# A decoder layer with an SSM branch on one core: the short convolution folded into the input projection on TensorE, the first projections placed ahead of it, and SP's queue reordered

## The reference, cut to what matters

```python
h  = layernorm(x)                        # 4 x 256 x 256
q, k, v = h @ Wq.T, h @ Wk.T, h @ Wv.T   # 32 query heads, 8 key heads of 64
q, k = rope(q), rope(k)
attn = softmax(causal(q @ k.T / 8)) @ v
x1 = x + attn @ Wo.T
# SSM branch on the context: 256 inner channels e
p  = in_proj_w @ ctx.T                   # 256 x 1024
xc[e, t] = sum(conv_w[e, j] * p[e, t - 3 + j] for j in range(4))   # within a sequence
u  = silu(xc + conv_b)
dt, Bm, Cm = split(x_proj_w @ u)         # 8, 16, 16 rows
delta = softplus(dt_proj_w @ dt + dt_proj_b)
state[e, n] = state[e, n] * exp(-exp(A_log) * delta) + delta * u * Bm[n]
y = sum_n(state * Cm) + D * u            # gated with silu(layernorm(x1)), added to x1
out = x2 + gated_ffn(layernorm(x2))      # 704 hidden channels, integer weights
```

## Time and profile before

| what | us |
|---|---|
| median of 3 runs | 524.07 (522.26 to 529.78) |
| the profiled execution | 523.78 |
| its span, first to last instruction | 522.0 |
| PE busy | 414.5 (79%) |
| DVE busy | 366.6 (70%) |
| ACT busy | 271.0 (52%) |
| POOL busy | 221.3 (42%) |
| mean granted TensorE clock | 0.912 of full |

### The profile page before, as it was taken

How to read it: one execution, slowest core, us unless ns; L and a number is a source line. 1 busy time by engine, 2 the same in 40 slices (tenths; PEclk the granted TensorE clock), 3 DMA queues, 4 the chain that set the end, 5 groups by cost and what they waited for, 6 DMA issues and landing times.

```text
span 522.0 us, 7681 instructions
## 1 busy us (share of the span) xinstructions
PE 414.5 (79%) x2604; PEld 325.4 (62%) x2636; DVE 366.6 (70%) x485; ACT 271.0 (52%) x779; POOL 221.3 (42%) x234
## 2 busy tenths in 40 slices
PE   3648987188768697987889799978998894659996
PEld 1433666166656476866777688757887773447774
DVE  2774357257999885897798679858767999755442
ACT  0514587046556465755666658645556665433321
POOL 1741232206464666446446635635464474310000
PEclk9787789687889799998999989989999997779999
DMA  9325324703151415201430521323042130000000
GB/s 223 74 56 96 113 51 131 230 10 98 37 170 55 156 31 153 96 11 46 133 102 24 144 91 48 76 87 102 21 133 74 57 102 0 2 0 21 20 22 20
DMA packets 51110, 40.63 MB, mean 78 GB/s; under 512 B 32280, under 2 KB 43744, under 8 KB 51072
## 3 DMA queue, kind: packets, MB, share of 16 engines
q1 hardware_dynamic: 40864, 34.48, 23.2%
q0 software_dynamic: 4096, 4.20, 3.4%
q10 hardware_dynamic: 6112, 1.47, 1.4%
HBM read 26.36 MB, written 1.18 MB: 53 GB/s over the span
## 4 chain that ended last, share of the span: by engine, by line
PE 33%; DVE 17%; issue 15%; SPq 12%; POOL 9%; DMA 7%; ACT 5%; ACTq 2%; DVEq 0%; POOLq 0%
PE ps_s L1041 6%; SPq L303 6%; PE ps_p L1028 6%; PE ps_p L1243 5%; DMA qt<-rc 4%; POOL rc L418 4%; DVE state L793 4%; PE ps_s L1228 3%; DVE nmax L711 3%; PE ps_p L1141 3%; PE ps_r L1095 3%; DVE state L786 3%; DMA kt<-rc 3%; SPq L266 2%; POOL y L424 2%
## 5 line engine op out<-in xcount | busy, mean ns | idle before, releaser
L493 ACT ACTIVATE prob<-ps_s,nmax 128x256 f32<-128x256 f32 (+1 forms) x256 | 104.8, 444 | 72.6 <-DVE nmax L711 72.6
L424 POOL TENSOR_TENSOR y<-y,state 128x1024 f32<-128x1024 f32 x32 | 80.3, 2510 | 112.2 <-DVE state L799 112.2
L418 POOL TENSOR_TENSOR rc<-rc,rs 128x512 f32<-128x512 f32 x40 | 57.7, 1442 | 104.0 <-DVE rs L699 70.4
L711 DVE TENSOR_REDUCE nmax<-ps_s 128x2 f32<-128x512 f32 (+1 forms) x96 | 60.3, 682 | 45.1 <-PE ps_s L1052 45.1
L499 ACT ACTIVATE pt<-ps_r 128x512 f32<-128x512 f32 x96 | 53.6, 593 | 58.1 <-PE ps_r L1095 54.5
L793 DVE TENSOR_TENSOR_SCAN state<-decay,state 128x1024 f32<-128x1024 f32 x32 | 81.5, 2546 | 2.3 <-ACT decay L519 1.2
L1041 PE MATMUL ps_s<-kt,qt 64*128 64x256 f32 (+1 forms) x512 | 55.5, 360 | 30.7 <-DMA qt<-rc 30.7
L1028 PE MATMUL ps_p<-xt_all,wq 128*128 128x256 f32 x256 | 71.2, 427 | 9.1 <-DVE rs L703 6.4
L1041 PEld LDWEIGHTS ps_s<-kt,qt 64*128 64x128 f32 x512 | 47.1, 201 | 38.2 <-DMA qt<-rc 32.5
L266 POOL DMA_DIRECT2D qt<-rc x128 | 63.8, 504 | 9.7 <-POOL rc L418 9.5
L1141 PE MATMUL ps_p<-wo,attn_t 128*128 128x256 f32 x256 | 61.7, 389 | 7.7 <-DVE x L816 4.1
(11 more groups left out here) (110 smaller groups left out, 531.1 us busy)
## 6 DMA issues: line engine op xcount, KB each, us to landing
bc<-bc_scratch SPq DMA_DIRECT2D x32, 512.0 KB, 4.7
qt<-rc POOLq DMA_DIRECT2D x128, 32.0 KB, 1.7
qt<-rc SPq DMA_DIRECT2D x128, 32.0 KB, 2.0
kt<-rc SPq DMA_DIRECT2D x64, 32.0 KB, 1.8
kt<-kt SPq DMA_DIRECT2D x8, 256.0 KB, 3.0
wo<-wo_t SPq DMA_DIRECT2D x1, 2048.0 KB, 10.9
wq<-wqkv_t SPq DMA_DIRECT2D x24, 64.0 KB, 2.6
xs<-x SPq DMA_DIRECT2D x1, 1024.0 KB, 8.1
```

Source lines behind the costliest of these rows:

```text
L418: nc.gpsimd.tensor_tensor(rc[:, r % 2, :, :], rc[:, r % 2, :, :], rs[:], ALU.add).then_inc(rope_add, 1)
L424: nc.gpsimd.tensor_tensor(y[:, v % 2, :], y[:, v % 2, :], state[:, v % 2, :], ALU.add).then_inc(state_free, 1)
L493: nc.scalar.activation(o, i, ACT.Exp, bias=nmax[:, r, c:c + 1], accum_out=rsum[:, r, GRP + head:GRP + head + 1]).then_inc(exp_done, 1)
L711: nc.vector.tensor_reduce(nmax[:, u % 2, c:c + k], ps_s[:, part, :].rearrange("p (k s) -> p k s", k=k), AX.X, ALU.max, negate=True).then_i ...
```

## The change

The four-tap convolution and the in-projection are both linear, so their weights are multiplied beforehand. POOL fills a matrix `ones` (instead of clearing the pad of the removed buffer). DVE scales the identity by each tap's weight (`diag`, 8 instructions of 128 x 128), PE multiplies `ones` by it, which puts each channel's tap weight in every row (2 matmuls of 512 columns, `row_ps`), and DVE multiplies that into the in-projection's weights (`taps`, 8 instructions). PE then convolves with four accumulating matmuls a bank, over the context shifted by 0 to 3 positions (16 matmuls of 506 to 512 columns), and ACT takes u straight from PSUM, with the bias, in four pieces of 512 columns. The in-projection, its copies, and the convolution on DVE and POOL go.

PE's order is now: tables, rows, x(0), x(1), k(0), q(0), x(2), x(3), conv(0), q(1), conv(1), v(0), scores(0), then as before. ACT's queue has `par` ahead of the tables and the eight pieces of wq behind the first activation. The k moves are shared, four issues by SP and four by POOL; the doubling is a step of its own (`double_k`), behind the next q move. SP's loop starts at unit 0, spreads the feed-forward loads over the units 4 to 8 and 11, and takes B and C for the scans of the unit before. On DVE, `prepare_scan(u)` runs ahead of the unit's scans; the dequantisations move to the units 10 and 14.

```diff
+        taps = early[:, 0:EB * DC * P].rearrange("p (e j n) -> p e j n", e=EB, j=DC)
+        diag = early[:, L:L + EB * DC * P].rearrange("p (e j n) -> p e j n", e=EB, j=DC)
+        ones = early[:, 2 * L:2 * L + P]
...
@@ sync
+            def double_k(j):
+
+                sp.wait_ge(k_sp[j % 2], 16 * k_moves * (j // 2 + 1))
+                sp.wait_ge(k_pool[j % 2], 16 * k_moves * (j // 2 + 1))
+                sp.dma_start(kt[HD:P, j % 2, :, :], kt[0:HD, j % 2, :, :]).then_inc(k_in[j % 2], 16)
...
-            move_k(0)
-            move_q(0)
-            move_q(1)
+            move_k(sp, 0, range(KG // 2), k_sp)
+            move_q(sp, 0, range(GRP // 2), q_sp)
+            double_k(0)
+            move_q(sp, 1, range(GRP // 2), q_sp)
...
             load_bc(0)
-            move_q(2)
-            load_wq(sp, 6)
-            load_wq(sp, 7)
-            move_q(3)
-            move_k(1)
-            sp.dma_start(wo[:], wo_t.rearrange("(k p) n -> p k n", p=P)).then_inc(wo_in, 16)
-            sp.dma_start(wgu_i[:], wgate_t.rearrange("(k p) n -> p k n", p=P)).then_inc(ffn_in, 16)
...
-            move_q(4)
-            move_q(5)
-            sp.wait_ge(ssm_ready, 5)
-            load_bc(1)
-            for u in range(4, UNITS):
+            for u in range(UNITS):
                 if u + 2 < UNITS:
-                    move_q(u + 2)
-                if u % KG == 1 and u // KG + 1 < GROUPS:
-                    move_k(u // KG + 1)
-                for v in scans(u):
+                    move_q(sp, u + 2, range(GRP // 2), q_sp)
+                if u % KG == 2 and u // KG + 1 < GROUPS:
+                    double_k(u // KG + 1)
+                if u < 2:
+                    load_wq(sp, 6 + u)
+                if u == 2:
+                    sp.dma_start(wo[:], wo_t.rearrange("(k p) n -> p k n", p=P)).then_inc(wo_in, 16)
+                load_ffn(u)
+                for v in scans(u - 1) if u else ():
                     if v % 2 == 1 and v // 2 + 2 < NS:
                         sp.wait_ge(hc_done, v + 1)
...
+                        load_bc(v // 2 + 2)
+                if u % KG == 1 and u // KG + 1 < GROUPS:
+                    move_k(sp, u // KG + 1, range(KG // 2), k_sp)
+                if u == 3:
+                    sp.wait_ge(ssm_ready, 5)
+                    load_bc(1)
...
@@ gpsimd
             add_rope(("k", 0))
+            move_k(nc.gpsimd, 0, range(KG // 2, KG), k_pool)
             add_rope(("q", 0))
...
                 if u % KG == 1 and u // KG + 1 < GROUPS:
                     add_rope(("k", u // KG + 1))
+                    move_k(nc.gpsimd, u // KG + 1, range(KG // 2, KG), k_pool)
...
@@ scalar
+            def silu_u(e):
+
+                for h in range(2):
+                    act.wait_ge(conv_ps, 2 * e + h + 1)
+                    src = ps_r[:, h, :] if e == 0 else ps_o[:] if h == 0 else ps_s[:, 2, :]
+                    nc.scalar.activation(u_s[:, e, h * 512:(h + 1) * 512], src, ACT.Silu,
+                                         bias=par[:, e, DC:DC + 1]).then_inc(u_done, 1)
...
@@ vector
+            for e in range(EB):
+                for j in range(DC):
+                    nc.vector.tensor_scalar(diag[:, e, j, :], ident[:], par[:, e, j:j + 1], None, ALU.mult
+                                            ).then_inc(diag_done, 1)
             dve.wait_ge(ln_rstd, 1)
...
+            for e in range(EB):
+                dve.wait_ge(row_ps, e + 1)
+                dve.wait_ge(ctx_in, 32)
+                for j in range(DC):
+                    nc.vector.tensor_tensor(taps[:, e, j, :], ps_s[:, e, j * P:(j + 1) * P],
+                                            inproj[:, e * P:(e + 1) * P], ALU.mult).then_inc(taps_done, 1)
             dve.wait_ge(tab_sb, 4)
             rope(("k", 0))
             rope(("q", 0))
-            convolve(0, slice(B // 2, B), conv_done0, DC)
             rope(("q", 1))
-            convolve(1, slice(B // 2, B), conv_done2)
             negmax(0)
...
+                if u < 4:
+                    prepare_scan(u)
                 for v in todo[:1]:
                     drive(v)
                     scan(v)
...
-                if u < 4:
-                    prepare_scan(u)
-                if u == 5:
+                if u == 10:
                     dequantise_gate()
-                if u == 12:
+                if u == 14:
                     dequantise_up_down()
...
@@ tensor
+            for e in range(EB):
+                pe.wait_ge(diag_done, DC * (e + 1))
+                nc.tensor.matmul(ps_s[:, e, :], ones, diag[:, e, :, :].rearrange("p j n -> p (j n)"),
+                                 start=True, stop=True).then_inc(row_ps, 1)
+
+            def convolve(e):
+
+                pe.wait_ge(taps_done, DC * (e + 1))
+                pe.wait_ge(ctx_in, 32)
+                pe.wait_ge(xt_sb, B)
+                for h in range(2):
+                    o = ps_r[:, h, :] if e == 0 else ps_o[:] if h == 0 else ps_s[:, 2, :]
+                    o = o.rearrange("p (b s) -> p b s", b=2)
+                    src = ctxs[:, h * 512:(h + 1) * 512].rearrange("p (b s) -> p b s", b=2)
+                    for lag in range(DC):
+                        last = nc.tensor.matmul(o[:, :, lag:], taps[:, e, DC - 1 - lag, :], src[:, :, 0:S - lag],
+                                                start=(lag == 0), stop=(lag == DC - 1))
+                    last.then_inc(conv_ps, 1)
...
                 if u == 0:
-                    pe.wait_ge(inp_sb, 2 * EB)
+                    pe.wait_ge(u_done, 2 * EB)
...
+            transpose_x(0)
+            transpose_x(1)
             fill(("k", 0))
             fill(("q", 0))
+            transpose_x(2)
+            transpose_x(3)
+            convolve(0)
             fill(("q", 1))
+            convolve(1)
             fill(("v", 0))
             scores(0)
```

More of the change, by code:

```diff
@@ L188, in decoder_layer @@
         wv_in = sem("wv_in")
-        q_in = [sem(f"q_in{r}") for r in range(2)]
-        k_half = [sem(f"k_half{r}") for r in range(2)]
+        q_sp = [sem(f"q_sp{r}") for r in range(2)]
+        q_pool = [sem(f"q_pool{r}") for r in range(2)]
+        k_sp = [sem(f"k_sp{r}") for r in range(2)]
+        k_pool = [sem(f"k_pool{r}") for r in range(2)]
         k_in = [sem(f"k_in{r}") for r in range(2)]
@@ L250, in load_wq, with move_q @@
                                         ).then_inc(wq_in[g], 16)
-        q_moves, k_moves = 2 * GRP, 2 * KG
-        half_moves = q_moves // 2
-        q_low = [sem(f"q_low{r}") for r in range(2)]
-        def move_heads(queue, u, heads, landed):
+        q_moves, k_moves = GRP, KG
+        def move_q(queue, u, heads, landed):
             r = ROPE_AT["q", u]
@@ L267, in move_heads, with move_k @@
                                     ).then_inc(landed[u % 2], 16)
+        def move_k(queue, j, heads, landed):
+            r = ROPE_AT["k", j]
+            queue.wait_ge(rope_add, r + 1)
+            if j >= 2:
+                queue.wait_ge(score_done, 3 * KG * (j - 1))
+            for i in heads:
+                for c in range(2):
+                    queue.dma_start(kt[c * HALF:(c + 1) * HALF, j % 2, i, :],
+                                    rc[i * HALF:(i + 1) * HALF, r % 2, c, :]).then_inc(landed[j % 2], 16)
         block = ctx.enter_context(nc.Block())
@@ L308, in _, with load_bc @@
-            move_k(0)
-            move_q(0)
-            move_q(1)
+            def double_k(j):
+                sp.wait_ge(k_sp[j % 2], 16 * k_moves * (j // 2 + 1))
+                sp.wait_ge(k_pool[j % 2], 16 * k_moves * (j // 2 + 1))
+                sp.dma_start(kt[HD:P, j % 2, :, :], kt[0:HD, j % 2, :, :]).then_inc(k_in[j % 2], 16)
+            def load_bc(n):
+                for c in range(2):
+                    sp.dma_start(bc[:, n % 2, c, :], bc_scratch[c * NS + n:c * NS + n + 1, :].to_broadcast([P, L])
+                                 ).then_inc(bc_in[n % 2], 16)
@@ new lines, in _, with load_ffn @@
+            full = P * (HT - 1)
+            def load_ffn(u):
+                if u == 4:
+                    sp.dma_start(wgu_i[:], wgate_t.rearrange("(k p) n -> p k n", p=P)).then_inc(ffn_in, 16)
+                elif u == 5:
+                    sp.dma_start(wdn_i[:, 0:HT - 1, :], wdown_t[0:full, :].rearrange("(k p) n -> p k n", p=P)
+                                 ).then_inc(ffn_in, 16)
+                    sp.dma_start(sdn[:], s_down.rearrange("(a n) -> a n", a=1).to_broadcast([P, HID])
+                                 ).then_inc(ffn_in, 16)
+                elif u == 6:
+                    sp.dma_start(wdn_i[0:HP[-1], HT - 1, :], wdown_t[full:HF, :]).then_inc(ffn_in, 16)
+                elif u in (7, 8):
+                    i, v = (0, s_gate) if u == 7 else (1, s_up)
+                    with nc.allow_non_contiguous_dma(reason="704 scales, once"):
+                        sp.dma_start(sgu[:, i, 0:HT - 1], v[0:full].rearrange("(k p) -> p k", p=P)
+                                     ).then_inc(ffn_in, 16)
```

(18 more changed lines are left out.)

111 lines of the change are left out of this document (22 added, 89 removed).

## The result

The kernel after took 485.22 us (median of 4 runs, 481.47 to 489.71) against 523.84 for the kernel before on the same chip: 0.922 of its time, 95% interval 0.912 to 0.932. Run again in five rounds it took 484.91 us, ratio 0.927 (0.923 to 0.932). The forecast was 497, with a range of 484 to 510: the sign is right, and the gain was forecast 12 us too small.

A forecast was written before the change was run, and what follows sets the result against it. No engine was full; TensorE's 30.7 us of waits for q moves, at the start, unit 3 and key groups, bound it. Terms -12.1 - 1.4 - 4.6 + 1.0 - 10.0 = -27.1 us from 523.78 gave 497 us, range 484 to 510.

The forecast's parts named there:

- The unit-3 stall: SP's queue in unit 3: q(4) issued ahead of doubling and loads removes PE's wait before unit 4's scores, -12.1 us.
- rival (d): Unit 4 not freed: another producer, the doubling or wo ahead of q(5), takes the stall over; 509 us, chance 0.06.
- The clock behind it: Scores of unit 4, after the wait: they run at full clock, 1.58 us instead of 2.93, -1.4 us.
- `prepare_scan`: DVE's unit: run before scans and reciprocals, it removes ScalarE's 3.66 us wait and shortens scores 5 to 6, -4.6 us.
- The start: Before the first scores: PE convolves at full clock while moves land, first scores at 42.9; +1.0 us, bounds -3 and +15.5.
- rival (c): The start: every convolution matmul runs at the lower clock, 14.5 us more; 511 us, chance 0.07.
- The key groups: Five group changes: shared k moves and q ahead of doubling shorten PE's waits, -10.0 us, bounds 0 and -16.8.
- B and C: SP's order: loads one unit later still arrive before DVE needs them; 0 us, bounds 0 and 2 us.
- (b): Key groups gain nothing, since POOL's four issues take what SP's half saves; 507 us, chance 0.15.
- (e): POOL's 32 k moves wait for DVE; slower than before, 570 us, deciding from 1.35 us per issue; chance 0.06.
- Dequantisation: Moved from units 5 and 12 to 10 and 14, same instructions; 0 us, bounds -2.9 and +2.9.
- rival (a): All five group waits and the lower clock behind them vanish, start 3 us shorter; 486 us, chance 0.15.

The follow-up runs named there:

- loads_bulk: Kernel after with the first doubling, wo and all feed-forward loads of units 4 to 8 in one piece ahead of q(4): 496.85 us, ratio 0.947.
- start_alone: Kernel before with the new start only; queue orders, k moves, prepare_scan and dequantisations as before: 522.31 us, ratio 0.997.
- queue_alone: Kernel after with the old start (in-projection with copies, convolution on DVE and POOL): 484.42 us, ratio 0.928.
- the k edit: Sharing the k moves between SP and POOL, plus doubling behind the next q move; undone in the kernel after: 483.6 us, ratio 0.924.
- bc_old: Kernel after with only the B and C loads back ahead of the next q move; k moves shared, doubling behind q: 484.6 us, ratio 0.925.
- k_by_sp: Kernel after with all eight k moves issued by SP; doubling still behind the next q move: 481.5 us, ratio 0.920.
- up_12: Kernel after with the dequantisation of up and down back in DVE's unit 12 instead of 14: 483.06 us, ratio 0.925.
- k_both_old: Kernel after with SP issuing all eight k moves and doubling at once; B and C still behind q: 483.6 us, ratio 0.924.
- bc_share: Kernel after with B and C and the doubling back ahead of the next q move, k moves still shared: 487.5 us, ratio 0.933.

## Why the prediction was right in sign and too small

**The unit-3 stall, -12.1: right.** The lead grew from 3.3 to 15.5 us there in the second profile, 12.2 us, and from 1.3 to 13.3, 12.0, in the first. loads_bulk gives back 11.9 in time for the stall and the clock behind it, where 13.5 were forecast. The reason stood as forecast: q(4) issued ahead of doubling and wo, and PE itself late next, with q(5) untouched by wo. I priced that as hidden at 0 and it was; rival (d) is out.

**The clock behind it, -1.4: right.** The scores ran in 1.58 us, and the distance 4 to 5 fell by 1.6.

**`prepare_scan`, -4.6: mechanism right, size too small.** I took 5.3 as the upper bound, since I measured the distance against the regular 8.9 us of later units; but units 4 to 6 have no output projection yet, and their free distance is 8.5. So the distance of scores 5 to 6 fell from 14.2 to 8.5, by 5.7 us. Putting the block back costs 7.3 us by unit 6 (0.9, 1.1 and 5.3 from the distances behind units 3, 4 and 5) and 8.7 in time: I had looked at the call with the longest wait, and booked 0.7 for one of those before it. Where the last us arises I haven't followed.

**The start, +1.0, and its clock: right as a sequence, 2.4 us off in size.** The forecast named 42.9 for the first scores, and they came at 40.49: the k fill began at 17.79 instead of 18.7, and what lies from there to the scores took 22.7 us instead of 24.2. The clock was granted as 1.00 from 16 to 46, and each convolution instruction took 0.44 us, so rival (c) is out. Windows of the kernel after (stretch, length, busy by engine, granted clock, DMA share, GB/s):

```profile
16.00:46.00 30.00, 28.77 (x107) 16.27 (x106) 8.28 (x20) 6.11 (x10) 9.99 (x15) 1.00 0.36 70
...
49.00:51.00 2.00, 2.00 (x5) 0.68 (x5) 1.53 (x3) 2.00 (x13) 0.00 (x0) 0.95 0.45 186
51.00:53.00 2.00, 2.00 (x6) 1.55 (x6) 0.70 (x2) 1.20 (x6) 0.00 (x0) 0.50 0.84 313
53.00:55.00 2.00, 2.00 (x11) 1.65 (x10) 0.50 (x1) 0.06 (x1) 0.00 (x0) 0.70 0.06 25
```

The scores and masks end at 42.4, where they had ended at 43.8: 1.4 us of gain in place of 1.0 of loss. Further on, the clock falls only at the end of dt_proj and not in its middle (3.95 us for its instructions instead of 5.33), which makes most of the rest of the 3.3 us of lead at unit 3. In the times the part is worth 1.4 us by start_alone's ratio (0.997 of 524; from 3.5 us of gain to 0.8 of loss) and nothing by queue_alone. The main step held: the 7.4 us of waiting were turned into convolution, not saved.

**The key groups, -10.0: the step that failed, by its size.** The gain was 15.9 us (13.7 in the first profile), near the bound of 16.8. The path itself came as forecast. At scores 12 POOL's sum of k ends at 168.85 and its sum of q at 174.75, 5.9 us later (forecast 5.6, with the four issues between); SP has issued q(12) by 177.35 and the doubling by 177.99, and PE waits 0.65 us, the 0.7 of the forecast. What failed is what I put on top of it. I doubled the 0.7 to 1.4 in case POOL's sums met DVE's work, and counted only 0.7 of gain at the two shorter waits. That let 6.8 of the 12.0 us of waiting stand; 2.2 are left, by the first row of after, none of them over 0.7. Read from the leads, the three long groups gave 7.2 us (forecast 4.5), the clock behind them 4.9 (4.8), and the two shorter ones 2.6 (0.7). The remaining 1.3 are no group's: the scores behind the second dequantisation come 4.65 us late, where they had come 5.95 late.

**B and C, 0: right beside the k edit, and blind to the rest.** bc_old has the loads ahead of q again and takes 484.6 us, so beside the k edit their move is worth nothing, as I had it (DVE once waited 0.30 us for them, at 137.92 in the first profile). But I asked only whether they came in time for their own user, and not what they did to the queue that they left. With the k edit undone the time is 483.6 us if the loads are moved, and 499.0 if they are not. The gain at the groups thus has two causes, each enough without the other: the k edit is worth 14.4 us if B and C stay and nothing if they move, and B and C 15.4 us if the k edit is undone and nothing beside it.

**Rivals (b) and (e): out.** (b) asked that the groups gain nothing, for 507 us; POOL's four issues stand where I put them, but k_by_sp, without them, is only 3.4 us below. For (e), the issues of POOL, by source line, q moves and k moves:

```profile
L267 POOL DMA_DIRECT2D qt<-rc x128: 498/503/836, 26.6 to 380.2; - x128
...
L278 POOL DMA_DIRECT2D kt<-rc x32: 498/500/713, 22.8 to 342.6; - x32
```

The longest took 0.84 us, so none came near the 1.35 from which (e) decides; the median, mostly beside DVE's scans, products and reductions, is 0.50.

"SBUF — State Buffer" (Trainium skill, section "SBUF: two separate sides") has GpSimd locked out of writing descriptors only while VectorE runs an instruction in a two-port mode. The prediction says that the trace of before does not bear this out; it hardly can, since no issue of POOL fell beside a `tensor_scalar` of DVE there. In the kernel after just one did, that at 67.3, beside those of `prepare_scan(1)` (two from 67.39, 1.29 us together), and it is the longest of the 128, in both profiles. That would agree with the Trainium skill; which mode they ran in, no row shows.

**Dequantisation, 0: right in the times** (up_12, within 2 us), with the 1.3 us above in the leads. **The tail** gives back 1.2 us that no step named.

**The sum, measured:** to unit 3 -3.3 (forecast +1.0), unit 4 -12.2 (-12.1), the clock -1.6 (-1.4), scores 5 to 11 -6.5 (-4.6), groups -15.9 (-10.0), tail +1.2 (0): -38.3 against -27.1. The largest error is the 5.9 us of the groups, the next the 4.3 ahead of unit 3, of which the times show less. What rival (a) named for 486 us, the group waits gone and a start 3 us shorter, is nearly what came; I gave it a chance of 0.15 because I had POOL's order against it. That order came true, but it left PE no more than 0.7 us of waiting at a group.

## What to carry to other kernels

Price a queue edit by the sum of what stands ahead of the move that someone waits for, bytes in flight as well as issues, and not edit by edit: here each of three edits was worth 7 to 15 us alone and nothing behind the two others, and a step moved "at nothing" because its own user is early could have freed the neighbour by itself. So undoing one edit shows what it adds to the others, not what it does; that takes a kernel without the others too. A block of work placed in a wait that its engine has anyway can pay at every call: here 5.3 us at one and about 1 at two more. Count them all, and take the free distance of the block's own stage as the floor. Work put on the engine whose wait it fills comes free only as long as the wait lasts: the whole convolution went where 7.4 us of waiting and the half clock had been, and leaving three quarters of it out gave 7 us at once.

## What the runs showed that I had not expected

**The clock fell under a busy engine.** In the windows above PE is busy 2.00 of 2.00 us in each stretch from 49 to 55, and yet the granted clock goes from 1.00 (2.4 GHz) to 0.50 (1.2 GHz) at about 51. What ran ahead of the fall are the 8 instructions of dt_proj, with 8 rows of contraction instead of 128, and 0.68 us of idle in front of them; the q fill behind them ran at half the clock. The kernel before shows the same: dt_proj from 48.42, a granted clock of 0.71 in the stretch 50 to 52 and of 0.50 in the next two, with PE busy throughout. In the first profile the fall came about 2 us earlier and lasted until past 58 (the matmuls took 5.76 us instead of 3.95), which makes the 2.8 us between the two profiles at unit 1. That the few rows of contraction are the cause was not tested.

**Landing time depends on what is in flight, whichever queue it came from:** 32 KB land in 1.8 to 2.0 us with nothing large under way (medians in the kernel after and k_both_old), and behind 1 MB of B and C, issued by SP, in 4.5 us from SP's queue and 4.2 from POOL's, at most 4.9 (bc_share).
